# The second residual of a selective-scan stage, added in the accumulation of the down product and copied out by ScalarE

## What is computed

```python
def _L0_attn_ref(x, ...):
    residual = x
    h = rmsnorm(x, w_norm1)
    z = h @ W_in.T
    z = z * jax.nn.sigmoid(h @ W_gate.T)
    y = selective_scan(z, W_xproj, W_dt, b_dt, A_log, D_skip)
    x = residual + y @ W_out.T
    hf = rmsnorm(x, w_ffn_norm)
    ffn = jax.nn.silu(hf @ W_gate_ffn.T) * (hf @ W_up.T) @ W_down.T
    return x + ffn
...
h = h + _L0_attn_ref(_layernorm(h, axis=-1), ...)
```

## Time and profile before

| | |
|---|---|
| device time, median of 3 (lowest to highest) | 1345.58 us (1344.37 to 1349.37) |
| the profiled execution, its own time | 1343.46 us |
| span of the profiled execution | 1341.6 us |
| mean granted TensorE clock | 0.942 |
| busy, share of the span | PE 88%, PEld 56%, DVE 80%, ACT 52%, POOL 55% |
| chain that ended last | PE 49%, DVE 24%, issue 11%, ACT 8%, POOL 6% |
| busiest groups | L1451 POOL 289.5 us, L1339 DVE 288.4 us, L1068 PE 245.7 us, L1207 ACT 212.7 us |
| the changed group, L1329 DVE | 16 instructions of 0.54 us |

### The profile page before, as it was taken

One profiled execution on the slowest core, in us unless ns is written; L12 is line 12 of the kernel. 1 busy time (PEld: TensorE's weight loads), 2 busy tenths in 40 slices (PEclk: granted clock), 3 DMA queues, 4 the chain that ended last, 5 costly groups with the idle time before them and its releaser, 6 DMA issues.

```text
span 1341.6 us, 19716 instructions
## 1 busy us (share of the span) xinstructions
PE 1185.7 (88%) x5716; PEld 755.1 (56%) x5717; DVE 1068.1 (80%) x2393; ACT 702.1 (52%) x1628; POOL 739.0 (55%) x465
## 2 busy tenths in 40 slices
PE   7986867578998989999977889999999889999996
PEld 4432434234454554545443568888888666776774
DVE  5999697899999999999999446687879556666663
ACT  1356431776877878786764345454544362332332
POOL 3147652778888797978884600144546565222222
PEclk9997878699999999999999899898989799999998
DMA  6200002651616243251520071001112133222221
GB/s 189 61 1 0 29 9 59 245 192 41 214 39 211 75 158 130 104 191 42 192 74 1 0 250 34 9 20 23 26 24 57 35 64 52 41 38 40 37 39 22
DMA packets 76913, 102.84 MB, mean 77 GB/s; under 512 B 13562, under 2 KB 65369, under 8 KB 76825
## 3 DMA queue, kind: packets, MB, share of 16 engines
q1 hardware_dynamic: 57490, 90.82, 20.5%
q0 software_dynamic: 17152, 9.24, 5.2%
q10 hardware_dynamic: 2184, 1.72, 0.5%
HBM read 70.23 MB, written 30.18 MB: 75 GB/s over the span
## 4 chain that ended last, share of the span: by engine, by line
PE 49%; DVE 24%; issue 11%; ACT 8%; POOL 6%; DMA 1%; DVEq 0%; SPq 0%; ACTq 0%; POOLq 0%
PE ps L2297 6%; DVE ps L1339 5%; PE ps L2275 5%; DVE hc L1351 5%; PE ps L1654 4%; PE ps L1068 4%; PE ps L2280 3%; PE ps L1712 3%; PE ps L1727 3%; PE ps L2287 3%; PE ps L277 2%; PE ps L270 2%; DVE ps L207 2%; ACT prod L398 2%; PE ps L982 2%
## 5 line engine op out<-in xcount | busy, mean ns | idle before, releaser
L1451 POOL TENSOR_TENSOR Bx<-dtz,BC 128x984 f32<-128x984 f32 x128 | 289.5, 2287 | 59.0 <-ACT u L1166 28.7
L1339 DVE TENSOR_TENSOR_SCAN ps<-ps,Bx 128x492 f32<-128x492 f32 x256 | 288.4, 1172 | 7.5 <-POOL Bx L1451 6.8
L1068 PE MATMUL ps<-hc,b_id 128*128 128x492 f32 x512 | 245.7, 608 | 42.8 <-DVE hc L1351 42.7
L1207 ACT ACTIVATE ps<-dt,A 128x324 f32<-128x324 f32 (+1 forms) x512 | 212.7, 457 | 52.5 <-DVE ps L1339 51.2
L1068 PEld LDWEIGHTS ps<-hc,b_id 128*128 128x128 f32 x512 | 92.2, 194 | 151.6 <-issue 104.8
L2433 POOL DMA_INDIRECT out<-yt,dest x48 | 74.7, 1556 | 158.4 <-DVE yt L2419 145.0
L2352 ACT ACTIVATE hT__7351<-ps,e_b 128x128 f32<-128x128 f32 x288 | 79.5, 374 | 153.6 <-PE ps L2287 153.4
L1351 DVE TENSOR_TENSOR hc<-ps,BC 128x656 f32<-128x656 f32 x224 | 139.2, 663 | 2.0
L2297 PE MATMUL ps<-W,hT__7351 128*128 x576 | 109.3, 327 | 0.9 <-DVE yb L2413 0.8
L2128 POOL DMA_INDIRECT buckets<-XS,c_slot x64 | 90.6, 1416 | 32.0 <-issue 16.4
L2140 POOL TENSOR_TENSOR c_x<-c_x,bro 82x192 f32<-82x192 f32 x32 | 18.9, 590 | 141.6 <-DVE c_x L1895 140.9
(11 more groups left out here) (283 smaller groups left out, 2418.1 us busy)
## 6 DMA issues: line engine op xcount, KB each, us to landing
BC<-bc_rows SPq DMA_DIRECT2D x16, 1312.0 KB, 9.5
BC<-bc_rows SPq DMA_DIRECT2D x28, 656.0 KB, 7.3
buckets<-b_zero SPq DMA_DIRECT2D x8, 2288.0 KB, 15.4
xg<-buckets SPq DMA_DIRECT2D x48, 104.0 KB
xc<-in_xcol SPq DMA_DIRECT2D x4, 1176.0 KB, 9.4
W<-in_w1d SPq DMA_DIRECT2D x8, 576.0 KB, 10.6
W<-in_w2d SPq DMA_DIRECT2D x8, 576.0 KB, 9.6
CL<-bc_rows SPq DMA_DIRECT2D x4, 656.0 KB, 8.3
```

What stands on the lines that cost most here:

```text
L1068: mm = pe.matmul(ps[:, BANK_Y + h, 0:HALF], ident[:], f2(hc[:, s % LONG])[:, h * HALF:(h + 1) * HALF], start=s == 0, stop=s == STATE - 1)
L1207: a = act.activation(ps[:, BANK_A + h, c:c + w].rearrange("p (g t) -> p g t", t=S)[:, :, 1:S], dt[:, (par + t // STATE) % 2, m, g0 * S:g1 ...
L1339: v.tensor_tensor_scan(hs[:, c], ps[:, BANK_A + h, 0:HALF], f2(Bx[:, t % RING])[:, c], 0.0, ALU.mult, ALU.add).then_inc(s_scan, 1)
L1451: g.tensor_tensor(Bx[:, t % RING], dtz[:, p], BC[:, t % STATE // GROUP, 0, t % GROUP, :].rearrange("p (a n) -> p a n", a=1).broadcast_to([ ...
```

## The change

VectorE's second add (`post` steps 14 and 15) is gone. TensorE opens the accumulation of each half with one product of the identity (82x82) and `x1` (82x384, both sequences of the half), and the 8 down matmuls of that half add to it; it now waits for `s_add` (GpSimd's `x1 + H`) ahead of the first. ScalarE copies both halves from PSUM to `H` in `post` step 15, which on ScalarE stands ahead of the decays of that step. In `ending` the calls move likewise.

```diff
@@ tensor, post
                 if s == 14:
+                    pe.wait_ge(s_add, p + 1)
                     pe.wait_ge(s_av, p * 4 + 4)
                     for h in range(2):
                         if not is_last(p):
                             free(f"N{h}", p, other)
+                        pe.matmul(ps[0:S, wide(f"N{h}", p), 0:2 * D], ident[0:S, 0:S], x1[:, 2 * h:2 * h + 2, :], start=True, stop=False)
                         for q in range(2):
                             c = (2 * h + q) * S
                             for k in range(NF):
                                 mm = pe.matmul(ps[0:S, wide(f"N{h}", p), q * D:(q + 1) * D], av[:, k, c:c + S], wdn[:, k, :],
-                                               start=k == 0, stop=k == NF - 1)
+                                               start=False, stop=q == 1 and k == NF - 1)
                         mm.then_inc(s_dn, 1)
@@ tensor, ending: the calls of post step 15 (empty on this engine) go
@@ scalar, post
+                if s == 15:
+                    for h in range(2):
+                        act.wait_ge(s_dn, p * 2 + (h + 1))
+                        act.activation(H[:, bass.ds(p * G + 2 * h, 2), :].rearrange("p j c -> p (j c)"), ps[0:S, wide(f"N{h}", p), 0:2 * D], ACT.Copy).then_inc(s_H, 1)
@@ scalar, ending
             def ending(last):
+                post(last - 1, 0, 15, None)
                 drain(last)
...
                 fr.keep_keys(act, 0, 0, 2, fr.place)
+                post(last, 1, 15, None)
@@ vector, post
-                if s in (14, 15):
-                    h = s - 14
-                    if h == 0:
-                        v.wait_ge(s_add, p + 1)
-                    v.wait_ge(s_dn, p * 2 + (h + 1))
-                    v.tensor_tensor(H[:, bass.ds(p * G + 2 * h, 2), :], x1[:, 2 * h:2 * h + 2, :],
-                                    ps[0:S, wide(f"N{h}", p), 0:2 * D].rearrange("p (j c) -> p j c", j=2), ALU.add).then_inc(s_H, 1)
@@ vector, ending
             def ending(last):
-                post(last - 1, 0, 14, None)
-                post(last - 1, 0, 15, None)
                 fr.stats(v, own, 0)
...
                 post(last, 1, 13, None)
-                post(last, 1, 14, None)
-                post(last, 1, 15, None)
                 v.wait_ge(s_H, 2 * ROUNDS + 2)
```

## The result

The changed kernel took a median of 1356.31 us (1347.21 to 1357.69, 4 runs) beside 1344.97 us before: ratio 1.0071, 95% interval 1.0046 to 1.0096. In a second set, run later beside 35 runs of before, it took 1349.09 us (1344.70 to 1357.28, 12 runs) beside 1344.11: ratio 1.0056, 1.0031 to 1.0082. So it is slower: by the ratios 7 to 10 us, by the medians 11.3 in the first set and 5.0 in the second. The profiled execution took 1355.21 us with a span of 1353.4 us; busy were PE 89%, PEld 56%, DVE 79%, ACT 52%, POOL 55%, at a mean granted clock of 0.942.

A forecast was written before the change was run, and what follows sets the result against it. The prediction took VectorE to bound the rounds, with TensorE's chain close behind and next. Rounds +6.0 and ending +3.3 made 9.3 us on 1343.46, so 1352.8, and 2.1 more for the median: 1354.9 us, range 1347 to 1359.

The forecast's parts named there:

- What bounds: Scan rounds: VectorE, 98% busy, bounds them; the chain over TensorE is close behind, slack 0.40 or 0.04 us ahead of `z`.
- The price of the identity product: TensorE behind the last `av`: four records of 384 columns at 0.32 us, 1.29 us a round, none hidden.
- The half price: Rival on TensorE's identity records: 0.16 us each, 0.65 a round, total 1349.8 us; chance 0.05.
- the lower bound: Lowest price of an identity record on TensorE, from the down product's 192-column records: 0.165 us, 0.65 a round.
- The copies: ScalarE's two 384-column copies from PSUM: 0.49 us each, bounds 0.44 and 0.99; decays behind late by 0.15 at most.
- The rounds: Scan rounds: `z` later by 0.92 or 1.28 us, rounds of 62.8 us, +6.0 us together.
- The ending: After the last scan: `hf` +2.05 us, last down product +1.29, less 0.06 at VectorE's add: +3.3 us.
- a rival of its own: TensorE's clock stays up in the ending through shorter idle spells: 6.5 us shrink to 3.8, total 1352.2 us; chance 0.12.
- The sign that I had named: TensorE in the ending: a clock other than half would show the forecast wrong.
- VectorE is the bound: Rival: TensorE has room, so the rounds give -3.9 us, the ending costs +3.3, about 1345.0 us; chance 0.12.
- The total: Whole kernel: 9.3 us more, 1352.8 us profiled, 1354.9 us as median, 0.7% slower; chance 0.58.

The follow-up runs named there:

- e1: Changed kernel with the identity product kept on TensorE, but VectorE instead of ScalarE copying the halves to `H`; 1346.61 us, ratio 1.0025.
- e3: Changed kernel with each identity product made twice, the second overwriting the first; 1358.03 us, ratio 1.0125.
- e2: Changed kernel without the identity products, ScalarE's copies kept, so `x1` is left out of `H`; 1337.91 us, ratio 0.9970.
- e5: Changed kernel with TensorE's gate products and product with `wx` one step earlier, in all rounds but the first; 1345.89 us, ratio 1.0015.
- v2: v1 with TensorE's gate products one step earlier as well; 1339.05 us, ratio 0.9969 to the kernel before.
- v1: Kernel before, but ScalarE copies the down product to `H` and GpSimd adds `x1`, except in the last two rounds; 1340.27 us, ratio 0.9980.
- e4: Changed kernel with the last drain ahead of ScalarE's two copies in the ending; 1350.31 us, ratio 1.0045.

## Why the prediction was right, point by point

- **What bounds.** VectorE at 98% was not the last word: the chain over TensorE had a slack of 0.04 to 0.40 us ahead of `z` in a round of 61.7. e1 and e3 show it by adding work there, e2 by taking VectorE's away.
- **The price of the identity product.** Forecast 0.32 us a record and 1.29 a round; the trace shows 0.65 us for two and the down product ending at 6.84 instead of 5.55. The half price falls for these records. The Trainium skill (TensorE: Matmul & The Clock Gate, Back-to-back issue gap) gives N/2.4 + 2.5 ns, an estimate of 163 ns for 384 columns; this trace has 325 ns at full clock and doesn't agree. A slip without effect: 5.40 / 32, the lower bound, is 0.169 us and not 0.165.
- **The copies.** Forecast 0.49 us, measured 0.47 and 0.49. The decays behind them were in time for the next scan, and the one after the drain, due at 502.87, came 0.09 us late (at most 0.15 forecast).
- **The rounds.** Forecast second `x1` add at 15.4, `z` at 23.26, rounds of 62.8 us, +6.0 us in all; measured 15.39, 23.27, 62.85 and +6.1 us. The waits were 0.74 (forecast near 0.9) and 0.55 us (0.6).
- **The ending.** +3.3 forecast, +2.6 measured between the first two profiles. `hf` was 1.9 us later (2.05 forecast). From `hf` to the last statistics the second residual's own +1.29 us were forecast, less 0.06, and it became 28.45 us instead of 27.80, +0.65. The missing 0.6 us is TensorE's clock, which I had kept as it was and had given a rival of its own. In the changed kernel TensorE (length, PE busy, granted clock):

```profile
760.00:763.20 3.20, 0.89 (x9) 1.00 0.00 0
763.20:770.00 6.80, 5.27 (x17) 0.50 0.00 0
```

  The stretch at half clock is 6.8 us, where in before it lasted 10.2 us (752.0 to 762.3), of which the earlier trace rows show a part. But the rival's reason, shorter idle spells, is not shown. e5 has the same ending: TensorE idled 1.45, 1.80 and 1.74 us ahead of the out product and the two groups of turns, the changed kernel 1.45, 1.80 and 1.75. Yet in e5 the stretch was as long as in before:

```profile
759.20:769.50 10.30, 7.88 (x22) 0.50 0.00 0
```

  There the last statistics came 48.80 us behind the last scan. And v2, whose ending is that of before, had 6.8 us and its last statistics at 44.37. So like compares with like: 47.73 - 44.37 = +3.4 us where both stretches are 6.8 us, 48.80 - 45.15 = +3.7 where both are 10.2 (+3.2 with v1, at 45.62, for before). The forecast +3.3 fits these; the +2.6 sets a short stretch beside a long one, and no run shows what decides between the two lengths. The sign that I had named, a clock other than half, did not appear; what changed was how long it was half.
- **The rivals.** "VectorE is the bound" needed a gap of 1.3 us between `av` and `z`; there is none, and e2 shows that even without the identity the chain is next: of the 3.9 us that VectorE saves, the scan stage gets 1.3. The Trainium skill's rule (Perfetto Trace Analysis, Identifying the Most-Contended Engine) to optimise the engine with the highest occupancy first led away from the answer here: VectorE's busy time did fall, from 121.4 us in 124 to 118.7, and the rounds grew.
- **The total.** 1354.9 forecast; 1356.31 in the first runs, 1349.09 in the second set. The sum of the first trace's own terms is 8.7 us beside the forecast 9.3. That the first median came within 1.4 us of the forecast is luck: its four runs spread over 10 us, and the second set's median is 7 us lower. The clock of the rest goes with that spread, and the prediction had no term for it; all it had right there is that the attention stage's work stays the same.

## What to carry to other kernels

Before moving work off the busiest engine, measure for each of its waits how far behind the other chain was: at 98% busy the second chain was 0.04 us away, and the work went onto it. Work that stood between the last operand and a gapless run of matmuls was paid in full here (e1, e3); an add given to an engine with gaps (GpSimd, v1) cost next to nothing. And put a copy that waits for late products behind, not ahead of, a drain that the next product needs (e4: 1.7 us at `hf`).

## What the runs showed that I had not expected

The same kernel's last 560 us took 563.4 us in one profile and 555.2 in another, with equal work and another granted clock; a difference of 0.001 in the run's mean clock went with 0.84 us. Changes of some 3 us can't be read from a few medians of this kernel, but they can from distances within the scan stage, which repeat to 0.1 us. Asking for TensorE's gate products a step earlier made TensorE wait for `z` and put `u` 1.1 us later behind the last `av` (v2 against v1), which cost GpSimd's inputs more than it gave.
